# Graph network and expert feed-forward kernel: expert weights loaded with 4 and 8 adjacent rows per partition, in transfers of 2 MB

## What is computed

```python
leaf = ...                      # per row: one of 16 experts, by four levels of a decision tree
onehot = jax.nn.one_hot(leaf, E_)
def body(acc, params):
    w1, bb1, w2, bb2, m = params          # w1 512 x 2048, w2 2048 x 512, float32
    h = jax.nn.gelu(xf @ w1 + bb1, approximate=False)
    y = h @ w2 + bb2
    return (acc + m[:, None] * y, None)
```

## Time and profile before

| | |
|---|---|
| median of 3 runs | 713.95 us (710.52 to 715.24) |
| profiled execution, its own time | 713.14 us |
| its span | 711.4 us |
| mean granted TensorE clock, share of full speed | 0.921 |
| TensorE matmul busy | 552.0 us (78%) |
| VectorE, ScalarE, GpSimd busy | 189.6, 162.4, 37.9 us |
| moved by DMA | 159.86 MB, mean 225 GB/s |

### The profile page before, as it was taken

How to read it: one execution, slowest core, us unless ns; L and a number is a source line. 1 busy time by engine, 2 the same in 40 slices (tenths; PEclk the granted TensorE clock), 3 DMA queues, 4 the chain that set the end, 5 groups by cost and what they waited for, 6 DMA issues and landing times.

```text
span 711.4 us, 9912 instructions
## 1 busy us (share of the span) xinstructions
PE 552.0 (78%) x2990; PEld 285.9 (40%) x2990; DVE 189.6 (27%) x573; ACT 162.4 (23%) x549; POOL 37.9 (5%) x37
## 2 busy tenths in 40 slices
PE   1708787889899999987899669667866877697960
PEld 1404455544456474444444334233323433341530
DVE  4746777381510201464011011001100110010101
ACT  0615777401102020020222021112111210121320
POOL 4000000020000000006200000000000000000003
PEclk9958999999999999999999898899998988998995
DMA  9933991000210010005999999999999999999805
GB/s 297 310 58 91 403 402 53 30 0 1 74 52 8 2 57 0 9 0 132 338 411 396 341 377 360 333 353 377 374 333 388 347 372 329 371 367 348 324 27 145
DMA packets 62951, 159.86 MB, mean 225 GB/s; under 512 B 12390, under 2 KB 15802, under 8 KB 53780
## 3 DMA queue, kind: packets, MB, share of 16 engines
q1 hardware_dynamic: 57360, 153.60, 59.5%
q0 software_dynamic: 3360, 3.86, 2.1%
q10 hardware_dynamic: 2212, 2.16, 0.9%
HBM read 145.04 MB, written 14.55 MB: 224 GB/s over the span
## 4 chain that ended last, share of the span: by engine, by line
PE 47%; DMA 19%; SPq 14%; DVE 5%; issue 5%; ACT 5%; POOL 2%; ACTq 1%; DVEq 0%; POOLq 0%
DMA w<-in_L_ffn_W 16%; PE P L860 11%; PE P L903 9%; PE P L766 7%; PE P L776 6%; SPq L349 4%; SPq L344 3%; PE P L785 3%; SPq L287 2%; ACT H L457 2%; ACT H L463 2%; SPq L271 2%; PE P L877 2%; SPq L265 2%; DMA xn<-y_rows,gidx 1%
## 5 line engine op out<-in xcount | busy, mean ns | idle before, releaser
L860 PE MATMUL P<-w,H 128*64 128x512 f32 x512 | 142.2, 705 | 60.1 <-DMA w<-in_L_ffn_W 58.4
L903 PE MATMUL P<-w,FB 128*64 128x256 f32 x1024 | 114.3, 381 | 0.0
L552 ACT ACTIVATE FB<-P,G 128x64 f32<-128x64 f32 x256 | 55.8, 329 | 216.9 <-PE P L877 195.5
L1242 DVE COPY H<-P 128x512 f32<-128x512 f32 x32 | 22.1, 692 | 296.8 <-PE P L860 296.8
L860 PEld LDWEIGHTS P<-w,H 128*64 128x64 f32 x512 | 40.9, 162 | 141.7 <-issue 106.7
L903 PEld LDWEIGHTS P<-w,FB 128*64 128x64 f32 x1024 | 72.0, 137 | 35.8 <-issue 0.3
L620 PE MATMUL P<-H 125*125 125x500 bf16 x176 | 59.4, 414 | 15.3 <-ACT H L463 12.8
L1003 DVE TENSOR_SCALAR H<-iota,small 125x626 bf16<-125x626 f16 x176 | 60.3, 383 | 27.1 <-issue 11.8
L766 PE MATMUL P<-G,XT 128*125 128x512 f32 x120 | 52.0, 592 | 0.0
L776 PE MATMUL P<-C,H 125*128 125x313 f32 (+1 forms) x160 | 42.4, 425 | 0.0
L620 PEld LDWEIGHTS P<-H 125*125 125x125 bf16 x176 | 25.2, 143 | 41.2 <-ACT H L463 27.0
(11 more groups left out here) (253 smaller groups left out, 394.4 us busy)
## 6 DMA issues: line engine op xcount, KB each, us to landing
w<-in_L_ffn_W SPq DMA_DIRECT2D x128, 1024.0 KB, 16.5
x_rows<-xn SPq DMA_DIRECT2D x5, 960.0 KB, 12.4
y_rows<-xn SPq DMA_DIRECT2D x5, 960.0 KB, 21.2
G<-in_L_gnn_W SPq DMA_DIRECT2D x3, 1024.0 KB, 5.4
XT<-x_rows SPq DMA_DIRECT2D x16, 128.0 KB, 17.1
y_rows<-XT ACTq DMA_DIRECT2D x16, 128.0 KB
xs<-in_x SPq DMA_DIRECT2D x1, 1120.0 KB
out<-xs SPq DMA_DIRECT2D x5, 224.0 KB
```

Of the source, the lines that this page charges most:

```text
L552: g = nc.scalar.activation(hT[:, m, :], P[:, 3 + rd, c * SA:(c + 1) * SA], ACT.Gelu, bias=bT[b][:, m:m + 1])
L860: mm = nc.tensor.matmul(P[g * SA:(g + 1) * SA, h, :], xT[b][:, k, :], w1a[:, k, h, g], start=(k == 0), stop=(k == KD - 1))
L903: mm = nc.tensor.matmul(P[g * SA:(g + 1) * SA, 7, 0:256], hT[:, m, :], w2_sb[b][:, m, g * 256:(g + 1) * 256], start=(m == 0), stop=(m == M ...
```

## The change

W1 is read so that partition p holds the four adjacent rows 4p to 4p + 3 (32 KB adjacent in HBM), in two transfers of two rows (16 KB per partition). Half h of W2 is read so that partition p holds eight adjacent rows (16 KB), in one transfer per half. So each expert is four transfers of 2 MB in place of eight of 1 MB. Because the partition of a row changes, three things follow: the input rows are turned with a stride of four columns (k-th of each four in place of the k-th block of 128); the hidden columns that TensorE turns together must be eight apart, so the first layer reads W1's columns in pieces of four adjacent ones out of each eight, VectorE's copy gathers every fourth column of PSUM into 128 adjacent ones, and gelu goes over the turned pieces in another order; and the bias table is turned to match. The W1 gate of SyncE is now after k = 1 and after k = 3, the W2 gates after each half.

```diff
@@ loads
-        b1_nat = G[:, 0:256].rearrange("p (h n) -> p h n", h=2)
+        b1_nat = G[0:2 * NE, 0:HID // 2]
-        s_w2 = [[sem(f"w2_in{b}_{q}") for q in range(4)] for b in range(2)]
+        s_w2 = [[sem(f"w2_in{b}_{h}") for h in range(2)] for b in range(2)]
...
-                for k in range(KD):
-                    sp.dma_start(w1_sb[b][:, k, :], W1[b, k * 128:(k + 1) * 128, :]).then_inc(s_w1[b], 16)
-                for q in range(4):
-                    sp.dma_start(w2_sb[b][:, 4 * q:4 * q + 4, :],
-                                 W2[b, q * DIM:(q + 1) * DIM, :].rearrange("(m p) n -> p m n", p=128)).then_inc(s_w2[b][q], 16)
+                for j in range(2):
+                    sp.dma_start(w1_sb[b][:, 2 * j:2 * j + 2, :], W1[b].rearrange("(p k) n -> p k n", p=128)[:, 2 * j:2 * j + 2, :]).then_inc(s_w1[b], 16)
+                for h in range(2):
+                    sp.dma_start(w2_sb[b][:, 8 * h:8 * h + 8, :],
+                                 W2[b, h * HID // 2:(h + 1) * HID // 2, :].rearrange("(p m) n -> p m n", p=128)).then_inc(s_w2[b][h], 16)
...
-                    for k in range(KD):
-                        if k < KD - 1:
-                            sp.wait_ge(s_w1u, (done - 1) * (KD - 1) + k + 1)
+                    for j in range(2):
+                        if j == 0:
+                            sp.wait_ge(s_w1u, (done - 1) * (KD - 1) + 2)
                         else:
                             sp.wait_ge(s_h, done * 2)
-                        sp.dma_start(w1_sb[b][:, k, :], W1[bass.ds(e, 1), k * 128:(k + 1) * 128, :].rearrange("a p n -> (a p) n")).then_inc(s_w1[b], 16)
+                        sp.dma_start(w1_sb[b][:, 2 * j:2 * j + 2, :],
+                                     W1[bass.ds(e, 1), :, :].rearrange("a (p k) n -> p (a k) n", p=128)[:, 2 * j:2 * j + 2, :]).then_inc(s_w1[b], 16)
...
-                    for q in range(4):
-                        sp.wait_ge(s_l2, 4 * (done - 1) + q + 1)
+                    for h in range(2):
+                        sp.wait_ge(s_l2, 4 * (done - 1) + 2 * h + 2)
+                        sp.dma_start(w2_sb[b][:, 8 * h:8 * h + 8, :],
...
@@ ScalarE
-                        g = nc.scalar.activation(hT[:, m, :], P[:, 3 + rd, c * SA:(c + 1) * SA], ACT.Gelu, bias=bT[b][:, m:m + 1])
-                        if c % 4 == 3:
+                    for j in range(8):
+                        m, c = 8 * rd + j, 2 * (j % 4) + j // 4
...
@@ TensorE
-                    t = nc.tensor.transpose(P[:, 6, k * SA:(k + 1) * SA], xr[b][:, k * 128:(k + 1) * 128], ident[0:SA, 0:SA])
+                    t = nc.tensor.transpose(P[:, 6, k * SA:(k + 1) * SA], xr[b].rearrange("s (p k) -> s k p", k=KD)[:, k, :], ident[0:SA, 0:SA])
...
-                w1a = w1_sb[b][:, :, :].rearrange("p k (h j g n) -> p k h g j n", h=2, j=4, g=2)
+                w1a = w1_sb[b][:, :, :].rearrange("p k (h n g r) -> p k h g n r", h=2, g=2, r=4)
...
-                    pe.wait_ge(s_w2[b][q], 16 * (p + 1))
+                    if q % 2 == 0:
+                        pe.wait_ge(s_w2[b][q // 2], 16 * (p + 1))
@@ VectorE
-                    nc.vector.tensor_copy(h_sb[:, t, :], P[:, t, :]).then_inc(s_hc, 1)
+                    nc.vector.tensor_copy(h_sb[:, t, :].rearrange("p (r n) -> p r n", r=4), P[:, t, :].rearrange("p (n r) -> p r n", r=4)).then_inc(s_hc, 1)
```

More of the change, by code:

```diff
@@ L180, in build @@
         sel = XT[:, 1792:1792 + NCH * SA].rearrange("p (c s) -> p c s", c=NCH)
-        b1_nat = G[:, 0:256].rearrange("p (h n) -> p h n", h=2)
-        b1T = G[:, 256:512]
-        bT = [G[:, 512 + b * MH:512 + (b + 1) * MH] for b in range(2)]
+        b1_nat = G[0:2 * NE, 0:HID // 2]
+        b1T = G[:, 1024:1280]
+        bT = [G[:, 1280 + b * MH:1280 + (b + 1) * MH] for b in range(2)]
         b2g = C[0:NC, :, 0:DIM]
@@ L321, in _ @@
             sp.wait_ge(s_gh, NCH * 3)
-            sp.dma_start(b1_nat, b1.rearrange("e (m p) -> (e m) p", p=128).rearrange("(h r) p -> r h p", h=2)).then_inc(s_b1, 16)
+            sp.dma_start(b1_nat, b1.rearrange("e (h n) -> (e h) n", h=2)).then_inc(s_b1, 16)
             def load_rows(b, i):
@@ L549, in tile_out @@
                     act.wait_ge(s_hT, 2 * i + rd + 1)
-                    for c in range(8):
-                        m = 8 * rd + c
+                    for j in range(8):
+                        m, c = 8 * rd + j, 2 * (j % 4) + j // 4
                         g = nc.scalar.activation(hT[:, m, :], P[:, 3 + rd, c * SA:(c + 1) * SA], ACT.Gelu, bias=bT[b][:, m:m + 1])
-                        if c % 4 == 3:
+                        if j % 4 == 3:
                             g.then_inc(s_gelu, 1)
@@ L557, in tile_out @@
                     for m in range(MH):
-                        g = nc.scalar.activation(hTB[:, m, :], P[:, 0, m * SB_:(m + 1) * SB_], ACT.Gelu, bias=bT[b][:, m:m + 1])
+                        c = 4 * (m % 4) + m // 4
+                        g = nc.scalar.activation(hTB[:, m, :], P[:, 0, c * SB_:(c + 1) * SB_], ACT.Gelu, bias=bT[b][:, m:m + 1])
                         if m % 4 == 3:
@@ L826, in _ @@
             pe.wait_ge(s_b1, 16)
-            for h in range(2):
-                t = nc.tensor.transpose(P[:, 5, h * 128:(h + 1) * 128], b1_nat[:, h, :], ident[:, :])
+            for r in range(8):
+                t = nc.tensor.transpose(P[:, 5, r * 2 * NE:(r + 1) * 2 * NE], b1_nat.rearrange("p (n r) -> p r n", r=8)[:, r, :], ident[0:2 * NE, 0:2 * NE])
             t.then_inc(s_b1T, 1)
@@ L842, in _ @@
                 for c in range(NCH):
-                    mm = nc.tensor.matmul(P[:, 6, k * SA:(k + 1) * SA], xn[0:NC, c, k * 128:(k + 1) * 128], sel[0:NC, c, :],
+                    mm = nc.tensor.matmul(P[:, 6, k * SA:(k + 1) * SA], xn[0:NC, c, :].rearrange("t (p k) -> t k p", k=KD)[:, k, :], sel[0:NC, c, :],
                                           start=(c == 0), stop=(c == NCH - 1))
@@ L853, in tile @@
                 pe.wait_ge(s_xTc, i + 1)
[L854 to L856 removed]
+                pe.wait_ge(s_w1[b], 32 * (p + 1))
+                w1a = w1_sb[b][:, :, :].rearrange("p k (h n g r) -> p k h g n r", h=2, g=2, r=4)
                 def first_a(h, k):
@@ L868, in first_b @@
                     for g in range(4):
-                        mm = nc.tensor.matmul(P[g * SB_:(g + 1) * SB_, 2, :], xTB[:, k, :], w1b[:, k, g],
+                        mm = nc.tensor.matmul(P[g * SB_:(g + 1) * SB_, 2, :], xTB[:, k, :], w1a[:, k, g // 2, g % 2],
                                               start=(k == 0), stop=(k == KD - 1))
@@ L931, in _ @@
             for k in range(KD):
-                t = nc.tensor.transpose(P[:, 2, k * SB_:(k + 1) * SB_], xrB[:, k * 128:(k + 1) * 128], ident[0:SB_, 0:SB_])
+                t = nc.tensor.transpose(P[:, 2, k * SB_:(k + 1) * SB_], xrB.rearrange("s (p k) -> s k p", k=KD)[:, k, :], ident[0:SB_, 0:SB_])
             t.then_inc(s_xTB, 1)
@@ L1224, in _ @@
             dve.wait_ge(s_b1T, 1)
-            nc.vector.tensor_copy(b1T, P[:, 5, 0:256]).then_inc(s_b1Tc, 1)
+            nc.vector.tensor_copy(b1T.rearrange("p (e r) -> p r e", r=8), P[:, 5, 0:256].rearrange("p (r e) -> p r e", r=8)).then_inc(s_b1Tc, 1)
             def copy_inputs(i, b):
@@ L1246, in tile_copies @@
                     dve.wait_ge(s_hB, 1)
-                    nc.vector.tensor_copy(h_sb[:, 2, :], P[:, 2, :]).then_inc(s_hBc, 1)
+                    nc.vector.tensor_copy(h_sb[:, 2, :].rearrange("p (r n) -> p r n", r=4), P[:, 2, :].rearrange("p (n r) -> p r n", r=4)).then_inc(s_hBc, 1)
                 if not (end and b):
```

3 lines of the change are left out of this document (1 added, 2 removed).

## The result

The changed kernel takes 730.49 us (median of 4 runs, 724.77 to 736.52), the kernel before 714.6 us in the runs beside it: a ratio of 1.0204, 95% interval 1.0163 to 1.0245. Run a second time it took 727.76 us (726.13 to 731.37), ratio 1.0212 [1.0169, 1.0255].

The account below looks back on a forecast made before the run. Two DMA engines carrying every store besides their weights bound the kernel; 16 KB packets starve stores, holding TensorE. 713.1 + 21 (holds) + 0.5 (VectorE copies) = 734.6, stated as 735 us; range 701 to 747.

Parts of the forecast that it names:

- The two engines bound the kernel before: Tile loop: the two DMA engines writing every store besides their weights set the pace, 24.1 us per tile.
- A 16 KB packet takes 620 ns: Weight loads after the change: 620 ns per packet on an engine, 32 per tile, 19.8 us.
- One for one at 16 KB: On the two store engines: one store packet per weight packet, so a store takes 42.6 us against a tile of 24.
- rival 1: Store queue: an engine gives the store more than one packet per turn, nothing holds TensorE; some 704 us; chance 20%.
- Stores 0 and 1 need 78 us: First two stores: 128 turns, 14 on row packets and 114 on weights; store 1 has left at 432, landed at 434.
- Tile 5 starts at 444: First hold: tile 3's copy waits for store 1, tile 4's second layer follows; tile 5 starts 16.5 us later than 427.5.
- Rounds of 24.6 us per tile: Tile loop after the first hold: rounds of four tiles in 98.5 us; nine tiles put tile 14 at 666, +21 us.
- From there TensorE bounds both, and all behind it stays: Tail from tile 14: TensorE sets the pace before and after, 43.2 us to the last copy, no change.
- First layer in pieces of four: 0: TensorE's first layer reading four of each eight columns: taken as 0, upper end +7.3 us per tile.
- VectorE's copies: +0.25 each: VectorE's stride-four PSUM copies: 0.25 us more per copy, two bare in the tail, +0.5 us.
- Turns of the bias table and strided turns: "under 1.5 us": More, smaller bias-table turns and strided turns of input rows: under 1.5 us, beside the scatter ahead of the loop; nothing.
- SyncE's blocked issues: worth nothing: SyncE's long weight issues disappear, with no gain in time because the two store engines' queue is never empty.

Follow-up runs that it names:

- the 512-byte store: Each store written as two transfers of 512-byte pieces on the same two engines: changed kernel 752.4 us, ratio 1.0532; kernel before 714.85 us, ratio 1.0001.
- the slower execution: The changed kernel, nothing altered, in the first of its two profiled executions: span 734.8 us, against 724.4 us in the second.

## Why the prediction was right

It said 735 us, by a store that two engines serve one packet per turn. The mechanism, its place and its sign are shown. The size was too large: it forecast 21.5 us more, and the two measurements have 15.9 (730.49 - 714.6) and 14.5 (727.76 - 713.3). Sizes within it were off both ways and partly cancel; that the total came within 7 us is partly luck.

- **The two engines bound the kernel before.** Right: relieving them alone gained 29 us, at a pace of 22.0 us per tile. The prediction used this only for the pace of the rivals.
- **A 16 KB packet takes 620 ns.** Right. The view by windows, a full stretch with no hold (columns: window, its length, busy time of PE, PEld, DVE, ACT, POOL, granted clock, DMA share, GB/s):

```profile
515.00:530.00 15.00, 15.00 (x106) 8.00 (x108) 1.20 (x3) 1.75 (x8) 0.00 (x0) 1.00 1.01 426
```

  426 GB/s over 16 engines make 16384 / 26.6 = 615 ns.
- **One for one at 16 KB.** Right: from 376 to 380.05 us the DMA view has 14 store packets, seven per engine, one every 0.58 us of the stretch, where 4.05 us hold six or seven weight packets:

```profile
q1 hardware_dynamic: 118, 1.67, 96.8%
q10 hardware_dynamic: 14, 0.01, 1.0%
```

  Of the Trainium skill's page DMA: Bandwidth & Descriptors, section Queues, rings and completion order, the prediction drew rival 1: whole packets of typically 9 to 17 descriptors before an engine switches. Here the measurement decides: 64 pieces of a store need about as many turns beside pieces of 2, 8 and 16 KB, not 4 to 7, and the 512-byte store doubles their number.
- **Stores 0 and 1 need 78 us.** Too long: 69. The step that failed is "some 14 fall on row packets, 114 on weights": at most some 108 were weight packets (the mean of 16 engines; the view doesn't part the two with the stores from the rest), so 20 turns or more fell on short ones. The same view has 12 row packets per engine and 272 pieces under 512 bytes, 17 per engine, most of them presumably the ones that close each transfer. If all of these take a turn, 99 are left for weights: 99 x 0.666 + 12 x 0.131 + 17 x 0.05 = 68.4 us, near the 69 measured. That is an estimate from these counts and the prediction's own prices, not a run of its own. The last packet left at 423.1 and the copy began at 424.20, 1.1 us behind it, where the prediction had 432 and 434.
- **Tile 5 starts at 444.** 437.50, and 442.20 in the slower execution. Of the +16.5 there were +10.0 (437.50 - 427.53). The landing came 10 us early, for the reason just named, and the steps behind it took 3.3 us more than said: 13.3 (437.50 - 424.20) in place of 10.0. Of that, 3.8 stand between the copy's start and the second layer (427.98 - 424.20), where 0.5 + 0.9 were taken; the issue of the next store, 1.01 us, lies in between and was left out. The second layer took 9.69 us, where 7.1 + 1.5 were taken. In the slower execution the loop had begun 6 us later.
- **Rounds of 24.6 us per tile.** Between the two executions: nine tiles from tile 5 to tile 14 take 212.3 us in one (649.77 - 437.50), 23.6 each, and 229.4 in the other (671.62 - 442.20), 25.5 each. In both, two held tiles follow each other and then come one to three at TensorE's own pace. The first held tile of each group is to be seen in TensorE's timeline, here of the execution of 724.4 us:

```profile
543.67 9.86 PE L908 MATMUL P<-w,FB 128*64 128x256 f32 x64 [10.77 <-ACT FB L556]
```

  and of the one of 734.8 us:

```profile
433.87 8.51 PE L908 MATMUL P<-w,FB 128*64 128x256 f32 x64 [16.18 <-ACT FB L556]
...
549.52 8.70 PE L908 MATMUL P<-w,FB 128*64 128x256 f32 x64 [10.43 <-ACT FB L556]
...
625.44 9.98 PE L908 MATMUL P<-w,FB 128*64 128x256 f32 x64 [6.47 <-ACT FB L556]
```

  Both begin with a round of five tiles in 115.7 us, 23.1 each (543.67 - 427.98; 549.52 - 433.87). Then one has a round of four in 95.9 (639.53 - 543.67), 24.0 each, the other one of three in 75.9, 25.3 each. The prediction had 24.6 for four and 25.1 for three: its pace per round holds, but it had every round as one of four.
- **"From there TensorE bounds both, and all behind it stays."** Wrong in the execution of 724.4 us, and this step hid part of the error of the others: tile 14 starts at 649.77, 16 us sooner than the 666 forecast. Its timeline at the tail:

```profile
639.53 9.72 PE L908 MATMUL P<-w,FB 128*64 128x256 f32 x64 [8.43 <-ACT FB L556]
...
649.77 4.51 PE L864 MATMUL P<-w,H 128*64 128x512 f32 x20
...
671.79 3.68 PE L908 MATMUL P<-w,FB 128*64 128x256 f32 x16 [8.70 <-ACT FB L556]
```

  From tile 14's start to the last copy it takes 51.6 us (701.38 - 649.77) in place of 43.2: tile 14 is held once more, by 8.70 us. The store that its ScalarE waits for, of tile 11, leaves only with the last weights at 666 us, and the copy of tile 13 follows at 667.14. The sum by this execution is +10.0 to tile 5, -5.1 over nine tiles (212.3 against 217.4, that is 644.95 - 427.53), +8.4 at the tail: +13.2 for the last copy (701.38 against 688.19). The other execution has +14.7, +12.0 and -2.2 at these steps.
- **First layer in pieces of four: 0.** Right. At full clock 20 matmuls take 4.46 us as before. Of the Trainium skill's page SBUF — State Buffer, section Door 1, the prediction took that four adjacent fp32 share a line and cost nothing: the trace agrees for the moving operand.
- **VectorE's copies: +0.25 each.** Nothing: 32 copies with a mean of 691 ns, 692 before.

```profile
L1247 DVE COPY H<-P 128x512 f32<-128x512 f32 x32 | 22.1, 691 | 294.8 <-PE P L864 294.8
```

- **Turns of the bias table and strided turns: "under 1.5 us".** Mis-sized: 4.9 us for the selector matmuls and 3.5 us for the turns of rows, the latter a quarter of a microsecond in TensorE's own pace (365.53 - 348.79 = 16.7, not 16.5). That they cost no time was right for the kernel before, where it was measured.
- **SyncE's blocked issues: worth nothing.** They are gone in the changed kernel: there an issue of half of W2 lasts 0.33 us in the median. But the prediction's reading that the pair of engines with the stores blocks them isn't borne out. Issues of a quarter of W2 in ns (least/median/longest), 400 to 645 us, in the kernel before and in the one with its store spread:

```profile
L349 SPq DMA_DIRECT2D w<-in_L_ffn_W x42: 384/3367/13408, 387.4 to 642.3; - x42
```

```profile
L349 SPq DMA_DIRECT2D w<-in_L_ffn_W x44: 444/3036/9026, 403.0 to 634.6; - x44
```

  With the store on all 16 engines the issues still last 3 us in the median. What ended the blocking is in the step from 2 KB to larger packets, an eighth as many; by what limit, no run shows.

## What to carry to other kernels

Before packets are made larger, count for each engine the packets of every queue that it serves: here a queue of small packets got one turn per large packet, so its latency grew with the size of its neighbour's packets while the engines moved no fewer bytes. Look first at how many engines a small store uses; here the order of two dimensions in its access pattern put it on two of 16, and spreading it was worth 29 us before and 57 to 59 us after the change. A buffer that waits for a store (two result tiles here) turns such a latency into a stall of everything that is queued behind the copy. More result tiles, the other remedy, were not tried.

## What the runs showed of the hardware

- An engine with a weight queue and a store queue gave a store packet about one turn per weight packet at 8 and at 16 KB; 64 packets took 20 us beside 8 KB and 34.5 us beside 16 KB. Packets of 512 bytes took a turn each as well.
- Weight loads of TensorE with a stride of four fp32 took 329 in place of 192 ns (125 rows) and 209 in place of 138 ns (64 rows), while the moving operand in runs of four fp32 and VectorE's PSUM copies with the same stride took no longer than before.
- With 128 packets per store and engine, the issue of a store while the one before was under way lasted 23.18 us in place of 1.70, with nothing named as the releaser. Issues of 1 MB in 2 KB packets lasted 3 us in the median, of 2 MB in 16 KB packets 0.33 us.
